# A two-layer graph network block in fp32: incidence and low-part records of the first steps made in halves

## The chip, the cores and the metric

One core of a Trainium2 chip. The time is device microseconds for one execution of the whole program; the median of several executions is compared. Five engines work beside each other and are ordered by semaphores: TensorE (PE), VectorE (DVE), ScalarE (ACT), GpSimd (POOL) and SyncE (SP, which issues most transfers).

## What is computed

For each of 16 graphs, with x of 512 x 256 and an adjacency matrix adj of 512 x 512 (all sizes fp32), two blocks follow each other, each added to its input:

```python
h = jnp.maximum(_layernorm(x), 0.0)
x = x + L0(h, adj)          # hypergraph convolution, relu, layer norm, convolution, + h
h = jnp.maximum(_layernorm(x), 0.0)
x = x + L1(h, adj)          # diffusion with attention, K = 3, relu

# inside L0
H = (adj != 0).astype(x.dtype)
w = adj.reshape(N, -1)[:, :C]
xw = jnp.einsum('ncd,hd->nch', x, W)
Dn = 1 / jnp.einsum('nce,ne->nc', H, w)          # 0 where the sum is not positive
Be = 1 / H.sum(axis=1)
m = Be[:, :, None] * jnp.einsum('nce,nch->neh', H, xw)
out = Dn[:, :, None] * jnp.einsum('nce,neh->nch', H, m) + b
```

H is the incidence matrix; the kernel needs it in two orders, as `inc` and transposed as `inct`. To keep fp32 accuracy, a factor of a product is held as a high part rounded for TensorE and a low part, the rest.

## The kernel before, in words

The work is a pipeline over the 16 graphs. Each engine runs the same steps k = -1 to 17, in `run_steps` (line 75 on); a step ends the second block of graph k - 2, does the beginning of that of k - 1 and the first block of k, and prepares k + 1. The steps k = -1, 0 and 1 are written out, k = 2 to 13 are a loop of 6 passes with two steps each (`eng.Fori`, line 86), and k = 14 to 17 are written out again. Every engine has its own copy of this loop and its own branch, recorded at L86. Nothing but semaphores ties the engines together, and the order of the work on each engine is the order in which the Python code issues it.

Step k = -1 is the opening of VectorE, `first_loads` (line 1483 on): statistics of x, then alternating one tile of `inc` (`incidence`, L1222) and one of `h_lo` (`h_lo_of`, L1476 to 1481), four of each, then the four tiles of the transposed incidence `inct` (`inct_tile`, L1485 to 1488, each as its transfer has landed), mixed with the reciprocals `be` (L1511 to 1513) and the low parts of m (`m_lo`, L1379, which write `part_b`). TensorE's `m_first` (line 1054 on) waits per tile for `inc`, for `h_hi` (made by GpSimd, L402) and for `h_lo`; its next products, at the top of step 0, wait for each tile of `inct` and of `part_b`. Step k = 0 is `first_step` (line 1529 on); it calls `h_lo_of` for four tiles, behind `y_lo` and ahead of `g_tile` (L1425), the whole `inct` of the next graph in one record (`inct_of`, L1437), the sums (L1207), `m_parts` (L1371 to 1379) and x1 (L1456). GpSimd makes `xt_lo` (L488; `g_lo` in the code, which shares its memory) behind additions of the skip term (L449).

In the loop h_lo is GpSimd's (L407), so that the changed functions are called in the steps k = -1 and k = 0 only, ahead of the loop. The first records of a pass on VectorE are those of `norm_x` (L1272 to 1287): a memset `landed` (L1279), eight `bn_aggr` into `mv_x` (L1281), two tiles of `inc`, and then `u_lo` (L1228), the low part of u, for which TensorE's products with `w_hi` and `w_lo` wait. The names `x`, `y`, `xl`, `e_sb` in the rows are x1, y10, xl or g_f, e_sb.

Of the kernel before, what the change touches and what calls it, by code (L numbers as in the profile page):

```python
# [27 lines left out]
P = 128  # L28
# [3 lines left out]
ALU = mybir.AluOpType  # L32
# [21 lines left out]
def at(s, ahead, tile=3):  # L54

    return s.k4 + (4 * ahead + tile + 1)
# [12 lines left out]
def wait(eng, sem, value):  # L69

    if not isinstance(value, int) or value > 0:
        eng.wait_ge(sem, value)
# [21 lines left out]
def build(nc, x, adj, adj_t, w1_t, b1, gamma, beta, w2_t, b2, wv_t, bv, aw, ab, wk, bk, out):  # L94
    NB, C, D = x.shape
# [8 lines left out]
    with ExitStack() as ctx:  # L104
        def sb(name, shape, dt):
            return ctx.enter_context(nc.sbuf_tensor(name, [P] + shape, dt))

        def sem(name):
            return ctx.enter_context(nc.semaphore(name))
# [8 lines left out]
        adjt_sb = sb("adjt_sb", [2, TI, C], F32)  # L118
        inc = sb("inc", [2, TI, C], F32R)
        inct = sb("inct", [2, TI, C], F32R)  # L120
        w_row = sb("w_row", [C], F32)
        h_f = sb("h_f", [TI, D], F32)
        h_hi = sb("h_hi", [TI, D2], F32R)
        h_lo = sb("h_lo", [TI, D], F32R)
# [103 lines left out]
        po_xb, h_hi_made, h_lo_made, po_skip, po_out, po_y0, po_plo, po_glo = (  # L228
            sem(n) for n in ("po_xb", "h_hi_made", "h_lo_made", "po_skip", "po_out", "po_y0",
                             "po_plo", "po_glo"))  # L230

        dv_inc, dv_inct, dv_hw, dv_a, dv_alo = (sem(n) for n in ("dv_inc", "dv_inct", "dv_hw", "dv_a", "dv_alo"))
# [13 lines left out]
        def f32(ap):  # L246

            return ap.bitcast(F32)
# [938 lines left out]
        def _(dve):  # L1187
            def step(s):
                q, o = s.par, 1 - s.par

                def stats_x(t, ahead):

                    if s.next2 if ahead == 2 else s.next:
                        if s.k == -1:
                            dve.wait_ge(ld_x0[t // 2], 16)
                        elif t == 0:
                            wait(dve, ld_x, dma_at(s, ahead - 1))
                        dve.bn_stats(st_x[:, t, :], xin[:, t, :]).then_inc(dv_stx, 1)

                def sums(t, s=s):  # L1200

                    if s.next:
                        if t == 0:
                            wait(dve, ld_wr, dma_at(s, 1))
                        wait(dve, dv_hw, at(s, 1, t - 1))
                        wait(dve, dv_inc, at(s, 1, t))
                        dve.scalar_tensor_tensor(hw[:, :], f32(inc[:, 1 - s.par, t, :]), 1.0, w_row[:, :], ALU.mult,  # L1207
                                                 ALU.mult, accum_out=dn_t[:, 0, t:t + 1]).then_inc(dv_hw, 1)
# [4 lines left out]
                def incidence(t):  # L1213

                    if s.next:
                        if s.k == -1:
                            dve.wait_ge(ld_a0[t], 16)
                        elif t % 2 == 0:
                            wait(dve, ld_a, half_at(s, 0, t // 2))
                        if t == 0:  # L1220
                            wait(dve, pe_g, at(s, -1))
                        dve.tensor_scalar(inc[:, o, t], adj_of(t), 0.0, None,  # L1222
                                          ALU.not_equal).then_inc(dv_inc, 1)
# [34 lines left out]
                def means_of_x(lo_t, hi_t):  # L1258

                    wait(dve, dv_stx, at(s, 1, hi_t - 1))  # L1260
                    dve.memset(landed_0[:, :], 0.0)
                    for t in range(lo_t, hi_t):
                        last = dve.bn_aggr(mv_x[:, t, :], st_x[:, t, :])
                    last.then_inc(dv_mvx, hi_t - lo_t)

                def shift_of_x(lo_t, hi_t):

                    wait(dve, po_rsx, at(s, 1, hi_t - 1))
                    dve.scalar_tensor_tensor(nb_x[:, lo_t:hi_t], mv_x[:, lo_t:hi_t, 0], -1.0, rs_x[:, lo_t:hi_t],
                                             ALU.mult, ALU.mult).then_inc(dv_nbx, hi_t - lo_t)  # L1270
# [105 lines left out]
                def m_lo(t):  # L1376
                    if s.next:
                        wait(dve, ac_m, at(s, 1, t))
                        dve.scalar_tensor_tensor(part_b[:, t, D:], ps0[:, t, 0:D], be[:, o, t:t + 1],  # L1379
                                                 f32(part_b[:, t, 0:D]), ALU.mult, ALU.subtract).then_inc(dv_mlo, 1)  # L1380
# [95 lines left out]
                def h_lo_of(t):  # L1476

                    wait(dve, ac_hf, at(s, 1, t))
                    wait(dve, h_hi_made, at(s, 1, t))
                    dve.tensor_tensor(h_lo[:, t, :], h_f[:, t, :], f32(h_hi[:, t, 0:D]),  # L1480
                                      ALU.subtract).then_inc(h_lo_made, 1)

                def first_loads():

                    def inct_tile(t):  # L1485
                        dve.wait_ge(ld_at0[t], 16)
                        dve.tensor_scalar(inct[:, o, t, :], adjt_sb[:, o, t, :], 0.0, None,
                                          ALU.not_equal).then_inc(dv_inct, 1)

                    stats_x(0, 1)  # L1490
                    stats_x(1, 1)
                    means_of_x(0, 2)
                    stats_x(2, 1)
                    stats_x(3, 1)
                    means_of_x(2, 4)
                    shift_of_x(0, 2)
                    incidence(0)
                    shift_of_x(2, 4)
                    h_lo_of(0)
                    incidence(1)  # L1500
                    h_lo_of(1)
                    incidence(2)
                    h_lo_of(2)
                    h_lo_of(3)
                    incidence(3)
                    inct_tile(0)
                    inct_tile(1)
                    for h in range(2):
                        pair = slice(2 * h, 2 * h + 2)
                        wait(dve, pe_m, at(s, 1, 2 * h + 1))  # L1510
                        dve.tensor_scalar(be_cnt[:, pair], ps0[:, pair, D], 1.0, None, ALU.max).then_inc(dv_bec, 2)  # L1511
                        dve.wait_ge(dv_bec, at(s, 1, 2 * h + 1))
                        dve.reciprocal(be[:, o, pair], be_cnt[:, pair]).then_inc(dv_be, 2)
                    inct_tile(2)
                    m_lo(0)
                    m_lo(1)
                    m_lo(2)
                    inct_tile(3)
                    m_lo(3)
                    dve.wait_ge(su_gb, 1)  # L1520
                    sums(0)
                    sums(1)
# [329 lines left out]
```

## Time and profile before

| | |
|---|---|
| median of 3 runs | 823.91 us (823.74 to 824.27) |
| the profiled execution | 824.95 us, of which the span of the records 823.2 us |
| mean granted TensorE clock | 0.997 of 2.4 GHz |
| TensorE busy | 806.8 us, 98% |
| VectorE busy | 640.3 us, 78%, 1740 records |
| chain that ended last | TensorE 85%, VectorE 6%, time with no cause shown 4% |

Times in the rows are microseconds from the first record. The idle time of an engine before a record stands in square brackets with what ended it; "issue" stands for no wait that the profile shows. A group of records xN that follow each other is one row, and since a record's end overlaps the next one's start, two take less than twice one. A q behind an engine's name is its sequencer, which handles branches, register operations and waits. The queue "q14 instruction" moves the program's own code.

### The profile page before, as it was taken

To read this page: it belongs to the slowest core of one execution; us is meant where nothing else is said; L and a number is where in the kernel's file an instruction comes from. 1 tells how busy PE (TensorE), PEld (TensorE's weight loads), DVE (VectorE), ACT (ScalarE), POOL (GpSimd) and SP (SyncE) were. 2 spreads that over 40 slices of the span, in tenths; PEclk is the share of its full clock that TensorE was granted. 3 is DMA by queue.
4 is the path that set the end of the run, shared out by engine and by line. 5 is a ranking of instruction groups with operands and counts; after the bars stand their busy time and mean duration, and the time that the engine had idled before them with its cause. 6 is when DMAs were issued, how large, how long until landed. Compare 5 with 4: busy or idle time off the path is not lost.

```text
span 823.2 us, 16671 instructions
## 1 busy us (share of the span) xinstructions
PE 806.8 (98%) x5750; PEld 751.5 (91%) x5750; DVE 640.3 (78%) x1740; ACT 474.6 (58%) x1005; POOL 429.6 (52%) x588
## 2 busy tenths in 40 slices
PE   7989999999999999999999999999999999999998
PEld 6878999999899989989899998998989999899997
DVE  6989878876878767878678787787877878786676
ACT  4438366572845728367383754747456483664745
POOL 2676573634738355482545736365473645832242
PEclk9999999999999999999999999999999999999999
DMA  9411204041130402204022130312204022020001
GB/s 299 124 64 52 91 15 153 2 137 32 42 124 0 166 2 76 89 0 166 2 76 90 33 133 2 121 45 76 89 2 160 6 76 90 13 91 1 26 2 52
DMA packets 39881, 58.03 MB, mean 70 GB/s; under 512 B 2576, under 2 KB 21008, under 8 KB 39824
## 3 DMA queue, kind: packets, MB, share of 16 engines
q1 hardware_dynamic: 39104, 57.42, 20.9%
q14 instruction: 40, 0.33, 0.1%
q8 instruction: 17, 0.28, 0.1%
q10 hardware_dynamic: 720, 0.01, 0.0%
HBM read 49.03 MB, written 8.39 MB: 70 GB/s over the span
## 4 chain that ended last, share of the span: by engine, by line
PE 85%; DVE 6%; issue 4%; POOL 2%; ACT 1%; DMA 1%; ACTq 0%; SPq 0%; DVEq 0%; POOLq 0%
PE ps L810 79%; PE ps L1035 3%; PE ps L965 1%; DVE x L1456 1%; PE ps L1011 1%; DVE y L1399 1%; DMA adj_sb<-in_adj 1%; DVE st_x L1462 1%; DVE inc L1222 1%; DVE part_a L1228 1%; DVE st_r L1331 1%; ACT h_f L591 0%; POOL skip L414 0%; POOL h_hi L402 0%; DVE mv_x L1281 0%
## 5 line engine op out<-in xcount | busy, mean ns | idle before, releaser
L810 PE MATMUL ps<-w_hi,part_a 128*128 128x256 f32 (+1 forms) x512 | 157.6, 342 | 6.8 <-DVE part_a L1228 4.2
L421 POOL TENSOR_TENSOR y<-y,bk_row 128x256 f32<-128x256 f32 x64 | 56.6, 914 | 199.3 <-DVE a_lo L1355 190.4
L810 PE MATMUL ps<-w_lo,part_a 128*128 128x256 f32 (+1 forms) x384 | 122.5, 319 | 0.0
L810 PEld LDWEIGHTS ps<-w_hi,part_a 128*128 128x128 f32 x512 | 96.2, 188 | 22.4 <-DVE part_a L1228 6.9
L810 PE MATMUL ps<-wk_hi,xt_hi 128*128 128x258 f32 (+1 forms) x256 | 89.4, 349 | 0.1
L810 PE MATMUL ps<-wk_hi,xt_lo 128*128 128x258 f32 (+1 forms) x256 | 86.7, 339 | 0.0
L810 PE MATMUL ps<-wk_lo,xt_hi 128*128 128x258 f32 (+1 forms) x256 | 86.6, 338 | 0.0
L810 PEld LDWEIGHTS ps<-w_lo,part_a 128*128 128x128 f32 x384 | 72.7, 189 | 5.4
L1349 DVE TENSOR_TENSOR e_sb<-e_sb,adjt_sb 128x512 f32<-128x512 f32 x64 | 44.2, 692 | 40.3 <-ACT e_sb L673 40.3
L810 PE MATMUL ps<-w_hi,part_b 128*128 128x256 f32 x256 | 72.4, 283 | 0.0
L488 POOL TENSOR_TENSOR xt_lo<-xl,xt_hi 128x256 fp32r<-128x256 f32 x60 | 56.1, 964 | 30.4 <-ACT xt_hi L747 30.4
L504 POOL TENSOR_TENSOR p_lo<-y,p_hi 128x256 fp32r<-128x256 f32 x64 | 45.6, 740 | 44.9 <-ACT p_hi L741 44.0
L741 ACT ACTIVATE p_hi<-y 128x256 fp32r<-128x256 f32 x60 | 24.0, 419 | 76.5 <-DVE y L1399 76.5
L810 PE MATMUL ps<-p_hi,a_hi 128*128 128x256 f32 x256 | 64.6, 286 | 0.0
L810 PE MATMUL ps<-y_hi,a_hi 128*128 128x258 f32 x256 | 64.4, 282 | 0.0
L810 PE MATMUL ps<-y_lo,a_hi 128*128 128x256 f32 x256 | 64.4, 282 | 0.0
L810 PE MATMUL ps<-xt_hi,inct 128*128 128x256 f32 x256 | 62.5, 285 | 1.5 <-POOL xt_lo L488 1.5
L734 ACT ACTIVATE part_b<-ps,be 128x256 fp32r<-128x256 f32 x64 | 28.4, 473 | 61.6 <-DVE be L1374 58.0
L810 PE MATMUL ps<-inct,part_b 128*128 128x512 f32 x256 | 62.5, 396 | 1.4 <-DVE part_b L1379 1.4
L810 PE MATMUL ps<-part_a,inc 128*128 128x256 f32 x512 | 62.6, 280 | 0.0
L810 PE MATMUL ps<-xt_lo,inct 128*128 128x256 f32 x256 | 62.1, 284 | 0.0
L810 PE MATMUL ps<-p_lo,a_hi 128*128 128x256 f32 x256 | 62.0, 281 | 0.0
(161 smaller groups left out, 2530.9 us busy)
## 6 DMA issues: line engine op xcount, KB each, us to landing
adj_sb<-in_adj SPq DMA_DIRECT2D x30, 512.0 KB, 5.9
adjt_sb<-in_adj_t SPq DMA_DIRECT2D x15, 1024.0 KB, 5.3
xin<-in_x SPq DMA_DIRECT2D x15, 512.0 KB, 4.6
out_dram<-x SPq DMA_DIRECT2D x15, 512.0 KB, 3.3
w_row<-in_adj SPq DMA_DIRECT2D x16, 256.0 KB, 3.5
adjt_sb<-in_adj_t SPq DMA_DIRECT2D x4, 256.0 KB, 7.1
e_sb<-in_w_t SPq DMA_DIRECT2D x2, 512.0 KB, 8.4
y<-in_wk SPq DMA_DIRECT2D x3, 256.0 KB, 7.0
```

What stands on the lines that cost most here:

```text
L421: pool.tensor_tensor(y10[:, t, D:], y10[:, t, D:], bk_row[:, :], ALU.add).then_inc(po_y0, 1)
L488: pool.tensor_tensor(g_lo[:, t, :], g_f[:, t, :], f32(g_hi[:, t, :]), ALU.subtract).then_inc(po_glo, 1)
L504: pool.tensor_tensor(p_lo[:, t, :], y10[:, t, 0:D], f32(p_hi[:, t, :]), ALU.subtract).then_inc(po_plo, 1)
L734: act.activation(part_b[:, t, 0:D], ps0[:, t, 0:D], ACT.Copy, scale=be[:, o, t:t + 1]).then_inc(ac_m, 1)
L741: act.activation(p_hi[:, t, :], y10[:, t, 0:D], ACT.Copy).then_inc(ac_p, 1)
L810: return pe.matmul(dst, stationary, moving, start=first, stop=last, skip_group_check=True)
L965: last = pe.transpose(ps0[:, t, col(2 * j + d)], xl[:, 2 * t + j, col(d)], ident[:, :])
L1011: last = pe.transpose(row[:, col(t)], column, ident[:, :])
L1035: last = pe.transpose(ps0[:, t, col(c)], r_sb[:, t, col(c)], ident[:, :])
L1222: dve.tensor_scalar(inc[:, o, t], adj_of(t), 0.0, None, ALU.not_equal).then_inc(dv_inc, 1)
L1228: dve.tensor_tensor(part_a[:, TD + d, :], ps0[:, d, :], f32(part_a[:, d, :]), ALU.subtract).then_inc(dv_ulo, 2)
L1349: dve.tensor_tensor(e_sb[:, t, :], e_sb[:, t, :], adjt_sb[:, o, t, :], ALU.mult).then_inc(dv_a, 1)
```

## The change

The low part of h in the two first steps, 128 x 256 for each tile, is subtracted in two halves of 128 columns, and each tile of the first transposed incidence, 128 x 512, is compared in two halves of 256 columns. The semaphore is raised by the second half. Four tiles of h_lo in k = -1, four in k = 0 and four of inct in k = -1: twelve records more on VectorE, all ahead of its loop. Nothing else differs.

```diff
                     wait(dve, ac_hf, at(s, 1, t))
                     wait(dve, h_hi_made, at(s, 1, t))
-                    dve.tensor_tensor(h_lo[:, t, :], h_f[:, t, :], f32(h_hi[:, t, 0:D]),
-                                      ALU.subtract).then_inc(h_lo_made, 1)
+                    for half in (slice(0, P), slice(P, D)):
+                        last = dve.tensor_tensor(h_lo[:, t, half], h_f[:, t, half], f32(h_hi[:, t, half]),
+                                                 ALU.subtract)
+                    last.then_inc(h_lo_made, 1)
 
                 def first_loads():
 
                     def inct_tile(t):
                         dve.wait_ge(ld_at0[t], 16)
-                        dve.tensor_scalar(inct[:, o, t, :], adjt_sb[:, o, t, :], 0.0, None,
-                                          ALU.not_equal).then_inc(dv_inct, 1)
+                        for half in (slice(0, C // 2), slice(C // 2, C)):
+                            last = dve.tensor_scalar(inct[:, o, t, half], adjt_sb[:, o, t, half], 0.0, None,
+                                                     ALU.not_equal)
+                        last.then_inc(dv_inct, 1)
```

## Rows read from the trace of the kernel before

**Rows 1.** The page: busy time of each engine; the instruction queue's packets.
```profile
PE 806.8 (98%) x5750; PEld 751.5 (91%) x5750; DVE 640.3 (78%) x1740; ACT 474.6 (58%) x1005; POOL 429.6 (52%) x588
...
q14 instruction: 40, 0.33, 0.1%
```

**Rows 2.** Windows, the loop's first two passes: length, busy us (records) by engine.
```profile
101.20:200.10 98.90, 98.90 (x716) 92.75 (x715) 78.67 (x214) 58.52 (x124) 53.57 (x72) 1.00 0.21 70
200.10:299.70 99.60, 99.02 (x714) 92.60 (x713) 77.73 (x213) 58.42 (x124) 53.70 (x72) 1.00 0.20 69
```

**Rows 3.** Timeline of VectorE, first record of the second pass (start, us, line, operation).
```profile
203.90 0.06 DVE L1279 MEMSET landed<- 128x1 f32 x1 [3.60 <-issue]
```

**Rows 4.** Waits of the whole span: us in total, times, longest.
```profile
DVE mv_x L1281 <- issue: 14.6, 4, 3.8
```

**Rows 5.** Timeline of VectorE, the same records inside the first pass.
```profile
151.16 0.78 DVE L1281 BATCH_NORM_AGGREGATE mv_x<-st_x 128x2 f32<-128x6 f32 x8
```

**Rows 6.** Timeline of TensorE at the start of the second pass.
```profile
206.00 0.49 PE L810 MATMUL ps<-w_hi,part_a 128*128 128x512 f32 x1 [0.58 <-DVE part_a L1228]
```

**Rows 7.** Records of line 86 from 196 to 204 us: ns, then first and last start.
```profile
L86 ACTq COMPARE_BRANCH  x1: 54/54/54, 197.5 to 197.5; - x1
L86 ACTq FUSED_REGOPS  x1: 44/44/44, 197.8 to 197.8; - x1
...
L86 DVEq COMPARE_BRANCH  x1: 72/72/72, 200.1 to 200.1; - x1
```

**Rows 8.** DMA view, windows 200.1:203.6, 203.6:206, 206:210, 250:254: packets, MB, share.
```profile
q14 instruction: 2, 0.02, 2.2%
...
q14 instruction: 1, 0.01, 1.1%
...
q14 instruction: 1, 0.01, 0.7%
...
q14 instruction: 1, 0.01, 0.9%
```

**Rows 9.** Groups by line and shape on VectorE: busy us, mean ns of one.
```profile
L1336 DVE TENSOR_TENSOR y_lo<-ps,y_hi 128x256 fp32r<-128x256 f32 x64 | 26.6, 422 | 16.7 <-ACT y_hi L602 16.4
L1228 DVE TENSOR_TENSOR part_a<-ps,part_a 128x512 fp32r<-128x512 f32 x32 | 21.8, 683 | 8.1 <-ACT part_a L558 8.1
...
L1437 DVE TENSOR_SCALAR inct<-adjt_sb 128x2048 fp32r<-128x2048 f32 x15 | 19.4, 1291 | 0.0
```

**Rows 10.** Timeline of VectorE in the step k = -1.
```profile
8.15 0.63 DVE L1480 TENSOR_TENSOR h_lo<-h_f,h_hi 128x256 fp32r<-128x256 f32 x1 [0.38 <-POOL h_hi L402]
...
9.25 0.60 DVE L1480 TENSOR_TENSOR h_lo<-h_f,h_hi 128x256 fp32r<-128x256 f32 x1
...
10.11 0.75 DVE L1480 TENSOR_TENSOR h_lo<-h_f,h_hi 128x256 fp32r<-128x256 f32 x2
...
11.12 0.75 DVE L1487 TENSOR_SCALAR inct<-adjt_sb 128x512 fp32r<-128x512 f32 x2
12.17 0.16 DVE L1511 TENSOR_SCALAR be_cnt<-ps 128x2 f32<-128x2 f32 x1 [0.30 <-PE ps L810]
```

**Rows 11.** Timeline of TensorE in the step k = -1 and at the top of step 0.
```profile
9.96 0.69 PE L810 MATMUL ps<-h_lo,inc 128*128 128x256 f32 x4
...
13.94 4.07 PE L810 MATMUL ps<-inct,part_b 128*128 128x512 f32 x16 [1.40 <-DVE part_b L1379]
```

**Rows 12.** Timelines of ScalarE and GpSimd in the step k = 0.
```profile
42.41 1.59 ACT L747 ACTIVATE xt_hi<-xl 128x256 fp32r<-128x256 f32 x4 [1.71 <-DVE xl L1425]
...
42.66 4.24 POOL L449 TENSOR_TENSOR skip<-xin,b_row 128x256 f32<-128x256 f32 x4
46.86 2.79 POOL L488 TENSOR_TENSOR xt_lo<-xl,xt_hi 128x256 fp32r<-128x256 f32 x4
```

**Rows 13.** Windows in the step k = 0; the third figure from the end is TensorE's granted clock.
```profile
47.00:50.50 3.50, 2.32 (x12) 1.69 (x13) 3.04 (x11) 2.78 (x5) 3.50 (x5) 0.99 0.63 217
50.50:53.90 3.40, 3.40 (x18) 3.40 (x17) 1.67 (x5) 0.00 (x0) 3.40 (x5) 0.50 0.22 85
```

## The prediction

> **What bounds the kernel now.** I read the page first. TensorE is busy for 98% of the span and VectorE for 78% [rows 1], so in steady state TensorE is the bound and the 12 added VectorE records cost nothing by being work. What matters is where TensorE waits. Two kinds of place are left: the opening, which runs once, and the way round the loop, which runs 6 times.
>
> The windows view, cut at VectorE's branches, gives the passes [rows 2]. In the first pass, which VectorE enters by falling into the loop, TensorE is busy all of 98.90 us. The second, entered by a jump back, has 99.60 - 99.02 = 0.58 us without a matmul. The timeline of VectorE says why: ahead of the first record of that pass stand 3.60 us that no semaphore explains [rows 3], and the list of waits has four more of the kind, 14.6 us together [rows 4]: all five jumps. The same records inside a pass, at 151.16, have no gap [rows 5]. TensorE has work queued and loses only 0.58 us, waiting for the low part of u (L1228) [rows 6]; the rest of the stall is covered.
>
> The DMA view says what the stall is. While VectorE stands still, two packets of the instruction queue are moved; one more follows as it resumes, one near 208 us, one near 251 us [rows 8]. Counting the loop's instructions in order, waits and register operations included, I get 284 per pass, about 292 records ahead of it, and these last two fetches fall about 28 and 156 instructions behind the head. They are 128 apart: the code comes in pieces of 128, the head lies 28 short of an edge, and the body covers 28 + 128 + 128 instructions, three pieces. ScalarE's body (169 instructions) covers two pieces, and its first instruction of the pass comes 0.3 us behind its branch at 197.5, where VectorE's branch at 200.1 is followed by the stall [rows 7]. So a jump finds its target still there when it goes one piece back, and not when it goes two.
>
> **The change, part by part.**
> *Length of the added records.* A subtract over 512 columns takes 683 ns and over 256 columns 422 ns [rows 9]: 0.26 us per 256 columns, and 128 columns should last 422 - 130 = 292 ns. The third and fourth h_lo together last 0.75 us where one lasts 0.41 [rows 10], so they start 0.34 us apart: 0.26 us of columns and 0.08 us fixed. A split adds one fixed part, 0.08 us. For the comparison, two of 512 columns last 0.75 us [rows 10], so 0.33 us from start to start, and 2048 columns 1291 ns [rows 9]: (1.29 - 0.42) / 3 = 0.29 us per 512 and about 0.05 us fixed. Where GpSimd works beside it, h_lo took 0.60 to 0.63 us [rows 10], so for those the fixed part is bounded by 0.05 below and 0.2 above. In all 8 x 0.08 + 4 x 0.05 = 0.84 us of VectorE, with ends of 0.5 and 2.0 us. No semaphore is raised by a first half, so no reader starts sooner.
>
> *The step k = -1 (four h_lo, four inct).* TensorE's products with h_lo(1) start at 9.96, 0.11 us behind the end of that record at 9.85 [rows 10, 11]: they go by VectorE, so the first two splits stand on the path, 2 x 0.08 = 0.16 us. h_lo(3) ends at 10.86 and is wanted after 11.4 (the four products per tile take 0.7 us from 9.96 on), which hides h_lo(2) and h_lo(3) in part; I take 0.05. VectorE idles 0.30 us before the first be_cnt at 12.17 [rows 10], which hides inct(0) and inct(1). inct(2) stands straight ahead of the part_b that ends TensorE's 1.40 us wait [rows 11]: 0.05 on the path. inct(3) is ahead of the last part_b, 0.05 more, half hidden behind the products of the others. Sum 0.3 us; with no cover it would be 0.52.
>
> *The step k = 0 (four h_lo).* They run in a row and end 0.32 us later. Behind them stand g, inct, the sums and m. What TensorE waits for is xt_lo on GpSimd, which starts at 46.86 only because four skip additions hold GpSimd from 42.66 [rows 12]; its input xt_hi is ready at 42.41 + 1.59 = 44.0. That cover is 2.9 us, against 0.32. The others feed TensorE only after its products with xt_lo, and wait under the same cover. What can show is that VectorE's longer use slows GpSimd beside it: 0 to 0.3 us, I take 0.1, as it is the same kind of neighbour that stretches h_lo from 0.42 to 0.6.
>
> *The loop.* No record of it changes, but all of it lies 12 instructions further on. The head is then some 16 short of an edge and the body covers 16 + 128 + 128 + 12, four pieces, or, should the head come to lie on the edge itself, 128 + 128 + 28, three. The jump back goes two or three pieces in either case, so the stall stays: 5 x 0.58 us for TensorE as now, nothing gained or lost. In the four-piece case one more fetch is asked for 11 instructions before the branch. Those 11 include four x1 and four statistics of 0.35 to 0.4 us each, so it is asked for some 3 to 4 us before the branch, about as long as the whole stall with two packets takes, and should cost nothing. Bounds: -0.58 us per pass (no stall) and, from the only row of a fetch, +2.6 us per pass (rival 1). Over five jumps -2.9 to +13 us; I take 0, as the count of pieces crossed is on the same side as now.
>
> *Sum.* 0.3 + 0.1 + 0 = 0.4 us. The profiled execution took 824.95 us for a span of 823.2, and would become 825.4. It stands 1.04 us above the median of the runs, 823.91, which would become **824.3**.
>
> **A rule weighed against this.** The rows show pieces of 8 KB (40 packets, 0.33 MB) at every 128th instruction [rows 1, 8]. The Trainium skill, "Runtime: NRT & Kernel Launch", section "Instruction fetch mechanics", speaks of an instruction memory of two blocks of 256 instructions for each engine but TensorE, of purely sequential prefetch, and of a taken branch that stalls when its target is outside that window. The trace agrees with the stall, not with the size of a piece. By that rule, if the edge behind the head is one of 256, the body now covers two blocks (28 + 256) and would cover three (16 + 256 + 12), with one more fetch to wait for at each jump; that is rival 1, and the sum would be its 837 instead of 824.3.
>
> **The rivals.**
> 1. *Slower: the head comes too close to the edge of what the jump fetches.* The mechanism: the two packets of the stall are one block, of which the head lies in the second half; what follows is the third packet, asked for on resuming. Now VectorE crosses the edge at about 207.3, behind a wait for GpSimd, and the piece is there. Twelve instructions sooner it crosses at about 204.5, beside the records that start with the jump [rows 3], and if a piece needs up to 3.5 us from asking (the stall itself) it is there at 203.6 + 3.5 = 207.1: up to 2.6 us of waiting ahead of u's low part, where TensorE has no slack left, times 5 = 13 us: 837. It decides as soon as the missing piece is later than 204.5. For it: nothing in the rows says which halves the two packets are. Against it: the stall waits for both packets, which makes sense if both are wanted, and only one is fetched on resuming. Chance 0.08.
> 2. *Faster: the stall shrinks or goes.* If the new position lets the jump hit, TensorE loses no 0.58 us at five jumps: 824.3 - 2.9 = 821.4. Against it: the body is longer than two pieces of 128 wherever it starts. Chance 0.14.
> 3. *Slower by the clock.* TensorE was granted 0.50 from 50.50 to 53.90, that is 1.2 GHz, and 0.99 (2.4 GHz) just before [rows 13]; before it fell, TensorE had been busy 2.32 of 3.50 us. Work at half the clock costs at most half of the 3.4 us, 1.7 us. Later work in the opening can add a second such stretch, 824.3 + 1.7 = 826.0, or lose this one, 822.6. Chance of one more 0.08, one less 0.04.
> 4. *Nothing shows:* every split hidden, 823.9. It lies in the forecast's own range.
>
> **How the numbers follow.** A measurement of this kernel can tell 0.2%, 1.65 us, from no change: outside 822.26 to 825.56. The forecast with rival 4 has 0.66, rival 1 0.08, rival 2 0.14, rival 3 0.12; of rival 3 the part with one stretch less stays within 0.2%. Faster: 0.14. Slower: 0.08 + 0.08 = 0.16, and 0.02 for the splits and contention at their upper ends, 0.18. Within: 0.68. The forecast's own range is 823.7 to 825.3 (all hidden; twice or three times my terms, towards the 2.0 us end). For 8 in 10 I go to rival 2's full gain below, 821.3, and to rival 3 with the splits' upper end above, 826.6; the 0.08 of rival 1 is left out.
>
> **What would show it.** In the changed profile: eight h_lo pairs near 0.25 to 0.4 us a record; TensorE's product with part_b(0) starting at 14.1 to 14.4, not 13.94; the gap at VectorE's jump 3.5 to 3.7 us in all five; TensorE's wait for part_a after it 0.5 to 0.8 us; instruction packets per pass five or six. The forecast is wrong if a second gap stands a few records behind the jump (rival 1), if the gap is missing or under 3 us (rival 2), or if the passes grow or shrink by more than 0.3 us.

## The result, and the profile after

The changed kernel takes **825.69 us** (median of 22 runs, 825.13 to 826.1), the kernel before 824.04 us in the same session (22 runs, 823.6 to 825.42): ratio 1.0019, interval 1.0012 to 1.0025. That is 1.65 us more, against 0.4 us in the prediction's sum; the time lies between the 821.3 and 826.6 that the prediction gave for 8 in 10, above its narrower 823.7 to 825.3, and at the edge of what it called no change (0.2%, 1.65 us). The profiled execution took 826.01 us, its span 824.2 us, 1.0 us more than the span before.

The page after, busy time and instruction queue (rows 1 are those of before):

```profile
PE 807.7 (98%) x5750; PEld 751.5 (91%) x5750; DVE 643.6 (78%) x1752; ACT 475.1 (58%) x1005; POOL 426.7 (52%) x588
...
q14 instruction: 40, 0.33, 0.1%
```

Twelve more VectorE records, as many instruction packets as before. I went on in the order of the prediction's steps.

**The opening.** Timelines of VectorE in the step k = -1, against [rows 10]:

```profile
8.25 0.72 DVE L1481 TENSOR_TENSOR h_lo<-h_f,h_hi 128x128 fp32r<-128x128 f32 x2 [0.74 <-POOL h_hi L402]
...
9.43 0.67 DVE L1481 TENSOR_TENSOR h_lo<-h_f,h_hi 128x128 fp32r<-128x128 f32 x2
...
10.37 0.88 DVE L1481 TENSOR_TENSOR h_lo<-h_f,h_hi 128x128 fp32r<-128x128 f32 x4
...
11.51 0.88 DVE L1490 TENSOR_SCALAR inct<-adjt_sb 128x256 fp32r<-128x256 f32 x4
```

Four halves together last 0.88 us where two whole ones last 0.75 [rows 10]: 0.065 us per split, near the 0.08 and 0.05 assumed. TensorE follows: its product with part_b(0) stands at 14.33 in place of 13.94 [rows 11].

```profile
14.33 0.47 PE L810 MATMUL ps<-inct,part_b 128*128 128x512 f32 x1 [1.47 <-DVE part_b L1379]
...
20.42 0.50 PE L810 MATMUL ps<-w_hi,part_a 128*128 128x512 f32 x1 [0.64 <-DVE part_a L1228]
```

Then comes something the prediction had not foreseen. The second of these two products started at 19.55 before:

```profile
19.55 0.50 PE L810 MATMUL ps<-w_hi,part_a 128*128 128x512 f32 x1 [0.22 <-DVE part_a L1228]
```

So TensorE is 0.39 us late at 14 us and 0.87 us late at 20 us. VectorE's timeline after shows the other 0.48: ahead of the second low part of u in step 0 it stands still with no semaphore to wait for, which it did not do before.

```profile
18.02 1.28 DVE L1530 TENSOR_TENSOR w_lo<-e_sb,w_hi 128x512 fp32r<-128x512 f32 x2
19.68 0.69 DVE L1228 TENSOR_TENSOR part_a<-ps,part_a 128x512 fp32r<-128x512 f32 x1 [0.37 <-issue]
```

From there to the loop the lateness stays where it is. In the step k = 0 the four h_lo take 3.35 us instead of 2.53, and TensorE's product with xt_lo, 47.63 before, comes at 48.52, 0.89 late: hidden, as predicted, though the four splits take 0.82 us more there and not the 0.32 of the prediction. The stretch at half clock [rows 13] is still there, 0.8 us later (granted clock 0.61 and 0.90 in the windows 50.50:53.90 and 53.90:58.00, where it was 0.50 and 1.00).

**The loop.** The list of waits after:

```profile
DVE landed L1279 <- issue: 10.3, 4, 2.7
DVE dn_t L1303 <- issue: 4.8, 5, 1.0
DVE mv_x L1281 <- issue: 2.5, 1, 2.5
```

Before, all five jumps cost VectorE one gap of up to 3.8 us [rows 4]. Now the gap at the jump is 2.5 to 2.7 us, and a second one of 1 us stands behind it. The timeline shows where:

```profile
203.71 0.06 DVE L1279 MEMSET landed<- 128x1 f32 x1
203.81 0.54 DVE L1281 BATCH_NORM_AGGREGATE mv_x<-st_x 128x2 f32<-128x6 f32 x7
204.27 0.73 DVE L1222 TENSOR_SCALAR inc<-adj_sb 128x512 fp32r<-128x512 f32 x2
205.92 0.17 DVE L1303 TENSOR_SCALAR dn_t<-dn_t 128x4 f32<-128x4 f32 x1 [0.92 <-issue]
```

The record at 205.92 is the 17th instruction behind the head. The DMA view of after gives one instruction packet in each of the windows 197:199, 201:203.4, 203.5:205.8, 205.8:208 and 248:250; the trace puts them at 197.80 (ahead of the branch at 200.66), 201.70 (in the first gap), 204.12 (0.62 us behind 203.50, where the sequencer's first instruction of the pass stands), 206.52 and 248.70.

What it costs TensorE is easily misread. The idle time the list shows is hardly more than before (3.2 us over five jumps, 3.1 before), because the end of a matmul is modelled. The starts tell it. Timelines of TensorE, first of before, then of after:

```profile
206.34 0.40 PE L810 MATMUL ps<-w_lo,part_a 128*128 128x512 f32 x1
206.57 0.64 PE L810 MATMUL ps<-w_hi,part_a 128*128 128x512 f32 x2
207.05 0.39 PE L810 MATMUL ps<-w_lo,part_a 128*128 128x512 f32 x1
```

```profile
207.22 0.40 PE L810 MATMUL ps<-w_lo,part_a 128*128 128x512 f32 x1
207.46 0.93 PE L810 MATMUL ps<-w_hi,part_a 128*128 128x512 f32 x2
208.22 0.40 PE L810 MATMUL ps<-w_lo,part_a 128*128 128x512 f32 x1
```

From the pair of products in the second row to the row behind it TensorE needs 0.48 us before (206.57 to 207.05) and 0.76 after (207.46 to 208.22): the second of the pair waits for the second low part of u as well, and no "idle" is shown. Measured against a pass without any gap (e2_shift28 below), the products behind the jump start 0.84, 0.80, 0.82, 0.91 and 1.03 us late before, 4.4 us in all, and 1.12, 1.30, 1.09, 1.29 and 1.07 us late after, 5.9 us: the loop costs **1.5 us** more. With the opening's 0.87 that makes 2.3 us. The profiled spans differ by only 1.0 because the profiled execution of before lost 1.4 us more further on, in three of its passes, and the one of after did not (in the one place that the list of waits shows, 0.34 us at 429.76, VectorE had waited 2.4 us for a late transfer of adj_sb; the others I did not trace). The medians differ by 1.65: less than 2.3, of which more under e1 and e4 below.

### The profile page after: what moved, and what is told of

Its sections match the earlier page's. It is cut to its first block, busy times and chain, and to the rows that moved or that the text cites. A ratio compares the mean times of both kernels' runs of the same rounds, so it can differ in the third digit from the quotient of the medians.

```text
span 824.2 us, 16683 instructions
## 1 busy us (share of the span) xinstructions
PE 807.7 (98%) x5750; PEld 751.5 (91%) x5750; DVE 643.6 (78%) x1752; ACT 475.1 (58%) x1005; POOL 426.7 (52%) x588
## 4 chain that ended last, share of the span: by engine, by line
PE 84%; DVE 8%; issue 5%; ACT 1%; POOL 1%; ACTq 0%; DVEq 0%; POOLq 0%
PE ps L810 78%; PE ps L1035 3%; PE ps L965 2%; DVE x L1456 1%; DVE inc L1222 1%; DVE y L1399 1%; PE ps L1011 1%; DVE st_x L1462 1%; DVE part_a L1228 1%; DVE st_x L1198 1%; DVE st_r L1331 1%; ACT h_f L591 0%; DVE mv_x L1281 0%; POOL skip L449 0%; DVE inct L1437 0%
```

## The experiments

Two theories of the loop went in. A *piece* is the 128 instructions that one packet of 8 KB brings by the prediction's count, and an *edge* is the border of two pieces; a loop is moved against the edges by instructions added or taken away ahead of it. *Theory A*: VectorE holds a few pieces of 128 instructions; the miss at the jump depends on how far the body reaches, in pieces, up to its branch; on a miss one piece is fetched, the next is asked for on resuming. *Theory C*, the prediction's: a jump over two pieces always misses. The tool for all of them is an instruction that only looks at a semaphore raised long ago, called a look below (two such waits in the code make one instruction, as the 12 more records of e1_shift12 for 24 waits show; 128 of them fill 9.9 us in e9_shift128, under 0.08 us each), put where VectorE idles 2.49 us in the step k = 1:

```diff
                 def p_out():

+                    if s.k == 1:
+                        for _ in range(2 * N):
+                            dve.wait_ge(ld_a0[0], 16)
                     wait(dve, pe_p, at(s, -1))
```

**Place of the loop alone.** N = 12, 28, 60 on the kernel before; and N = 16 on the changed kernel, whose loop then stands where N = 28 puts it.

> The kernel before, with 12 instructions that only look at a semaphore raised long ago, put on VectorE ahead of the row sums of the step k = 1, where VectorE idles 2.49 us. No split. It tells place from work. Theory A (a jump fetches one piece of 128 instructions, and the next is asked for on resuming): the opening is as before, TensorE at 19.55 us starts the same product as before; at the five jumps VectorE has a gap of 2.7 to 2.9 us instead of 3.5 to 3.7 and a second one of 0.9 to 1.1 us some 17 instructions behind the head; time 823.9 to 824.7 us. Theory B (the loop's second gap comes from the halves themselves): no second gap, first gap 3.5 us, 824.0. If the whole slowdown of 1.65 us were the place of the loop: 825.7.

> The same with 28 instructions, which puts the loop's head on the edge of a piece and the body into three pieces. Theory A, with the sharper claim that a jump over two pieces hits when VectorE has not looked into a fourth: no gap at any of the five jumps, TensorE's 0.55 to 0.77 us at each are gone, about 3 us less, 821 us. Theory C (three pieces are always too many, the jump over two always misses): first gap 2.8 to 3.6 us at each jump, no second gap since 128 instructions follow before the next edge, 824.0.

> The same with 60 instructions: the head 32 instructions behind an edge, the body again in three pieces, its branch in the middle of the third. Theory A: no gap at the jumps, 821 us; should the 60 looks last longer than the 2.49 us that VectorE idles there, up to 2 us are lost once. Theory C: gap of 2.8 to 3.6 us at each, 824.0 to 826.

> The changed kernel, halves and all, with 16 such instructions at k = 1, so that its loop stands where that of e2_shift28 does. It gives the halves' own cost in the opening, with the loop's place held. Theory A: 0.9 us above e2_shift28 (0.39 from the halves at k = -1, 0.48 from the wait of 0.37 us ahead of u's low part in k = 0), so about 822. Theory C: 0.9 us above e2_shift28 at 824, so about 825. If the halves cost nothing: equal to e2_shift28.

The kernel before took 823.86 us beside these four.

| | us | ratio to before (interval) |
|---|---|---|
| e1_shift12 | 824.79 | 1.001 (1.0001 to 1.0019) |
| e2_shift28 | 819.08 | 0.9944 (0.9930 to 0.9957) |
| e3_shift60 | 818.80 | 0.9938 (0.9924 to 0.9952) |
| e4_halves_shift16 | 819.73 | 0.9950 (0.9937 to 0.9964) |

Twelve looks make the changed kernel's loop without a single split. The waits of e1_shift12:

```profile
DVE landed L1279 <- issue: 7.8, 3, 2.7
DVE mv_x L1281 <- issue: 5.0, 2, 2.5
DVE dn_t L1303 <- issue: 4.9, 5, 1.1
```

Its passes lose 1.17, 1.07, 1.27, 1.36 and 1.06 us, 1.5 us more in all than before loses at its jumps. The median rose by only 0.93. In the profile of e1 the window that ran at half clock before [rows 13] ran at full clock, and the first product with part_a behind it started at 59.41 instead of 59.83:

```profile
50.50:53.90 3.40, 3.40 (x27) 3.21 (x26) 2.79 (x8) 0.00 (x0) 3.40 (x5) 1.00 0.20 77
```

But that is not why the rise is small: the runs of either kernel whose mean granted clock was 1.000 differ by 0.9 us as well (medians 824.64 and 823.74). What fits is that the median run of before also loses something behind its jumps, as its profiled run did: it stands 4.78 us above e2_shift28, where its jumps cost 4.4, and e1 stands 5.71 above, where its jumps cost 5.9. No trace of such a run was taken, so this is not shown.

With 28 looks the gap is gone. The page of e2_shift28, its window over the second pass, and VectorE's timeline at the jump:

```profile
q14 instruction: 15, 0.12, 0.0%
```

```profile
199.63:298.18 98.55, 98.55 (x714) 92.50 (x713) 78.62 (x213) 58.51 (x124) 53.47 (x72) 1.00 0.21 69
```

```profile
199.43 0.74 DVE L1465 BATCH_NORM_STATS2 st_x<-x 128x6 f32<-128x256 f32 x2
200.30 0.06 DVE L1279 MEMSET landed<- 128x1 f32 x1
```

No instruction packet is moved from 196 us to the end of the loop, 15 in the whole run instead of 40, and a pass takes 98.55 us where [rows 2] have 99.60. Windows over the same five passes, cut at TensorE's branches, for before, after and e2_shift28, one after the other:

```profile
196.71:695.22 498.51, 495.02 (x3563) 462.78 (x3562) 388.15 (x1061) 292.18 (x621) 268.75 (x360) 1.00 0.21 69
```

```profile
197.61:696.25 498.64, 495.30 (x3563) 462.31 (x3561) 389.94 (x1061) 292.42 (x621) 266.04 (x360) 1.00 0.21 69
```

```profile
196.58:689.31 492.73, 492.73 (x3563) 462.50 (x3561) 393.26 (x1061) 292.52 (x621) 267.27 (x360) 1.00 0.21 69
```

Before takes 5.8 us more than e2_shift28, 4.4 of them at the jumps and 1.4 behind them; only 3.5 were visible as idle time of TensorE. Theory C, and with it the prediction's picture of the jump, falls: this body spans three pieces and its jump over two of them hits. Theory A holds, but I had sized the gain from the idle time, at 3 us; it is 4.8 us in the medians. Run e4 gives what the halves cost with the loop's place held: 0.65 us above e2 in the medians, where 0.9 was expected. These medians mix runs that had a stretch at half clock with runs that had none (the profiled e2 had one, the profiled e4 none). Among runs of the same mean granted clock it is 0.76 us (819.62 and 818.86, at 1.000) and 0.95 us (820.07 and 819.12, at 0.998), which fits the 0.87 us of the timelines. By the medians the change's 1.65 us is thus the loop's 0.93 (e1) and the opening's 0.65 (e4), 1.58 together.

**Where exactly it tips, and the opening.** e5 puts the loop between before and e1. e6 moves it one instruction the other way (the merged record below saves two, one look adds one):

```diff
-                    for t in range(TI):
-                        h_lo_of(t)
+                    h_lo_of(0)
+                    h_lo_of(1)
+                    wait(dve, ac_hf, at(s, 1, 3))
+                    wait(dve, h_hi_made, at(s, 1, 3))
+                    dve.tensor_tensor(h_lo[:, 2:4, :], h_f[:, 2:4, :], f32(h_hi[:, 2:4, 0:D]),
+                                      ALU.subtract).then_inc(h_lo_made, 2)
```

e7 adds eight records and no halves, ahead of the first statistics (20 looks hold the loop):

```diff
+                    for i in range(8):
+                        dve.memset(spare[:, i:i + 1], 0.0)
                     stats_x(0, 1)
```

e8 has the halves at k = -1 only (`if s.k == -1` around the choice of halves, 20 looks).

> The kernel before with 5 instructions that only look at a raised semaphore, at k = 1 on VectorE, between before (0) and e1_shift12. The body now reaches 5 instructions into a fourth piece and the edge lies 23 behind the head. Theory A (one piece fetched on a miss, the next asked for on resuming and usable some 2.3 us later): the fetch of the fourth piece starts about 1 us ahead of the branch, so the gap at the jump shrinks to 2.7 to 3.1 us as in the changed kernel, and VectorE reaches the edge 23 behind the head only 2.2 us after resuming, so the second gap is nearly gone (0 to 0.3 us). TensorE then loses 0.1 to 0.4 us per jump in place of 0.8 to 1.0 (before) and 1.1 to 1.3 (after): 820.5 to 822.5, so better than both. Theory D (every position that misses costs the same): 824.0 to 824.8.

> The kernel before with its loop 1 instruction earlier: in k = 0 the subtract of h_lo(2) and h_lo(3) is one record over both (2 instructions fewer, in a stretch that waits for GpSimd anyway), and 1 look at k = 1. The branch that closes the loop is then the last but one slot of its third piece, where in the kernel before it is the last. Theory A with the sequencer looking one instruction ahead: no gap at the jumps, 819.1 as e2_shift28. If it looks two or more ahead: gap of 3.5 us, 824.0. Theory E (the kernel before misses because its head is far into a piece, not because of where its branch lies): 824.0.

> The kernel before with 8 small memsets of a spare tile ahead of the first statistics of k = -1, where VectorE waits for x until 3.78 us, and 20 looks at k = 1, so that the loop stands where that of e2_shift28 does. No halves: the records of k = -1 and 0 take as long as before but lie 8 further on. It asks whether the wait of 0.37 us ahead of u's low part (k = 0) in the changed kernel comes from the place of the code. If from the place (edge of a piece right ahead of that record): that wait is there, TensorE is 0.48 us later from 20 us on but not at 13.94, time 819.5 (0.5 above e2_shift28's 819.1). If from the halves' own length: no such wait, 819.1.

> Halves only at k = -1 (four h_lo, four inct: 8 more records), none at k = 0; 20 looks at k = 1 hold the loop where e2_shift28 and e4_halves_shift16 have it. If the halves at k = 0 are hidden, as predicted: equal to e4_halves_shift16, 819.7, with TensorE 0.39 us later from the product with part_b(0) and 0.87 us from 20 us on. If the halves at k = 0 cost what VectorE spends on them (0.8 us): 0.3 to 0.8 us below e4_halves_shift16.

The kernel before took 823.74 us beside these.

| | us | ratio to before (interval) |
|---|---|---|
| e5_shift5 | 819.72 | 0.9951 (0.9937 to 0.9965) |
| e6_shift_minus1 | 819.09 | 0.9945 (0.9932 to 0.9959) |
| e7_early8 | 819.56 | 0.9949 (0.9936 to 0.9963) |
| e8_halves_first_step | 819.81 | 0.9956 (0.9943 to 0.9970) |

e6: one instruction earlier, and the gap is gone at all five jumps, with 15 instruction packets. So the kernel before misses because its branch is the very first position that touches the fourth piece (it stands in the last place of the third piece, and the instruction behind it is the first of the fourth). e5: the jump misses, but the list of waits shows why it hardly costs anything:

```profile
DVE landed L1279 <- issue: 12.6, 5, 2.7
...
DVE dn_t L1308 <- issue: 0.4, 1, 0.4
```

The first gap is short as in the changed kernel, since the packet for the fourth piece is moved 2.4 us ahead of the branch and no longer beside the one for the head, and the second is almost gone, since VectorE gets to the edge, 23 behind the head, when the piece is just there. TensorE loses 0, 0, 0.16, 0 and 0.16 us. The cost of a position is not a step but a curve: 0 for -1, 0.9 us per jump for 0, 0.1 for +5, 1.2 for +12.

e7: the wait in straight code comes from the place. VectorE's timeline, with no halves anywhere:

```profile
17.68 1.28 DVE L1532 TENSOR_TENSOR w_lo<-e_sb,w_hi 128x512 fp32r<-128x512 f32 x2
19.35 0.69 DVE L1229 TENSOR_TENSOR part_a<-ps,part_a 128x512 fp32r<-128x512 f32 x1 [0.39 <-issue]
```

TensorE is 0.1 us late at 14 us and 0.54 at 20 us, and the time is 0.48 us over that of e2 (of another session, whose kernel before took 0.12 us more). The place can also be counted. I take VectorE's records in order from the first, its sequencer's included, and go back in steps of 128 from the edge that e6 found at the loop's branch: an edge lies ahead of the 64th record. In the changed kernel, e4, e7 and e8 the 64th is this low part of u, with 0.37 to 0.39 us ahead of it; in the kernel before, e1, e2, e3, e5, e6, e9, e10 and e12 it is a small record of dn_t at 20.9 to 21.3 us, and u's low part has no such gap. (In e11, below, it is the other low part of u.) e8: 819.81 beside e4's 819.73, so the four splits at k = 0 cost nothing that shows.

**Period, nearness, and two more versions.** N = 128 and N = 14 on the kernel before; the changed kernel with four early memsets and 12 looks; and the opposite of the change, one record over all four tiles of h_lo at k = 0 with six instructions fewer:

```diff
-                    for t in range(TI):
-                        h_lo_of(t)
+                    wait(dve, ac_hf, at(s, 1, 3))
+                    wait(dve, h_hi_made, at(s, 1, 3))
+                    dve.tensor_tensor(h_lo[:, :, :], h_f[:, :, :], f32(h_hi[:, :, 0:D]),
+                                      ALU.subtract).then_inc(h_lo_made, 4)
```

> The kernel before with 128 looks at k = 1: its loop lies exactly one piece of 128 further on. It asks whether the places repeat every 128 instructions or every 256. If every 128 (theory A, pieces of 128): the gap of 3.5 us stands at all five jumps as in the kernel before, no second gap, TensorE 0.8 to 1.0 us later per jump; the looks themselves last about 7 us where VectorE idles 2.49, so once up to 4.5 us are added: 824 to 828.5. If every 256: no gap at the jumps, 819 to 823.6.

> The kernel before with 14 looks: the head 14 instructions short of the edge, two nearer than in e1_shift12. Theory A: the first gap 2.7 us, the second some 15 instructions behind the head and a little longer (1.0 to 1.3 us), TensorE 1.1 to 1.5 us later per jump: 824.8 to 825.5. If the head is put on the edge itself when it comes this near to it: no gap at all, 819.1.

> The changed kernel, all halves, with 4 small memsets ahead of the first statistics of k = -1 and 12 looks at k = 1, so that the loop stands where that of e4_halves_shift16 does and all records of the opening lie 4 further on. If the wait of 0.37 us ahead of u's low part comes from the place of the code alone, the edge now falls ahead of the second product with w_row before it or the subtract for w1_lo, where VectorE has little slack either: the wait moves to one of them. If it then hides: no such wait, TensorE 0.4 us later than before from 20 us on instead of 0.87, 819.3. If it shows there as well: 819.7 as e4_halves_shift16.

> The other way round from the change: in k = 0 the four subtracts of h_lo are one record over all four tiles (6 instructions fewer), nothing else. The loop comes 6 instructions earlier, its branch 7 slots short of the end of its third piece. Theory A: no gap at any jump, 819.1 (818.7 to 819.5), better than both kernels. If only a position at the very edge of a piece hits: 824.0.

These four ran on a chip where the kernel before took 825.05 us, so their ratios count.

| | us | ratio to before (interval) |
|---|---|---|
| e9_shift128 | 832.34 | 1.0089 (1.0073 to 1.0105) |
| e10_shift14 | 833.73 | 1.0093 (1.0059 to 1.0127) |
| e11_halves_early4 | 820.02 | 0.9941 (0.9927 to 0.9955) |
| e12_merged_h_lo | 819.53 | 0.9938 (0.9924 to 0.9952) |

e9 behaves at the jumps as the kernel before does. Its waits:

```profile
DVE ri_t L1395 <- issue: 40.4, 14, 9.9
DVE landed L1279 <- issue: 11.0, 3, 3.8
DVE mv_x L1281 <- issue: 7.4, 2, 3.8
```

Five long gaps and no second one; TensorE loses 1.02, 1.06, 0.91, 0.82 and 0.82 us. The places repeat every 128 instructions. The total missed its bracket because of the looks and the clock: the looks make a gap of 9.9 us instead of 2.49 in the step k = 1, more than the 7 I had allowed, TensorE stands idle for 4.95 us, and behind that its clock falls to the lower level for 6.8 us, so that 16 products with inct take 6.81 us instead of 3.89. Both are paid once:

```profile
105.00:111.80 6.80, 6.17 (x15) 4.83 (x16) 6.65 (x27) 2.19 (x5) 3.97 (x6) 0.50 0.00 0
```

e10 was the largest miss of the experiments: I expected the second gap to grow by 0.1 to 0.3 us, and the time by 1 us. Timeline of VectorE, then windows of TensorE behind the jump (the third figure from the end is the granted clock):

```profile
202.88 0.55 DVE L1281 BATCH_NORM_AGGREGATE mv_x<-st_x 128x2 f32<-128x6 f32 x7
205.10 0.78 DVE L1222 TENSOR_SCALAR inc<-adj_sb 128x512 fp32r<-128x512 f32 x2 [1.67 <-issue]
```

```profile
205.20:207.20 2.00, 0.02 (x2) 0.02 (x1) 2.00 (x7) 0.00 (x0) 2.00 (x4) 1.00 0.02 4
207.20:210.60 3.40, 3.40 (x10) 2.66 (x11) 3.40 (x10) 2.69 (x6) 1.36 (x3) 0.62 0.00 0
210.60:214.00 3.40, 3.40 (x15) 2.71 (x14) 2.14 (x5) 2.02 (x4) 3.15 (x6) 0.88 0.00 0
```

Two instructions nearer, the edge stands ahead of the incidences and no longer behind them. In e1 these 0.7 us of work are done while the piece is on its way; here they come after it, and the first dn_t lasts 0.68 us instead of 0.17. TensorE then idles 2.0 us, and behind that idle time its granted clock fell to the lower level (0.50, 1.2 GHz) from 208.0 to 211.4 us, and likewise behind the other four jumps. TensorE's first product starts 2.1 to 2.2 us late, and in the stretch at half clock it loses 1.6 us more: 3.8 us per jump in the profiled run, whose time was 837.97 and whose mean granted clock was 0.990. Of the four runs two were like it (836.41 too), and two took 831.05 and 829.92 us with a mean granted clock of 0.998, too high for five such stretches. So the clock does not fall behind every such jump.

e11 moved the wait in straight code and did not remove it: with all records four further on it stands ahead of the other low part of u, where it is lumped with a wait for ScalarE.

```profile
17.74 0.69 DVE L1229 TENSOR_TENSOR part_a<-ps,part_a 128x512 fp32r<-128x512 f32 x1 [0.72 <-ACT part_a L559]
```

e12, with no padding at all, takes 5.5 us less than the kernel before on the same chip (0.6%), and so is faster than both kernels, as e2, e3 and e6 are.

## Why the prediction was right, and where not

**The splits: right.** The sum had 0.3 us for k = -1, measured 0.39 at 14 us; 0.1 for k = 0, measured nothing (e8 beside e4), under the cover of GpSimd's additions that the prediction named. Together 0.4, as put. VectorE's own extra time at k = 0 was mis-sized, 0.82 us and not 0.32; the cover of 2.9 us hid either.

**The range: right by luck.** The total of 0.4 us was a quarter of the 1.65 measured, and two parts of that, the loop and the wait in the opening, the sum had at nothing. The time fell inside 821.3 to 826.6 because its upper end had been set for a second stretch at half clock, which did not come. By the prediction's own signs the forecast was wrong: a second gap stands behind each jump, and the first is under 3 us.

**The opening's other 0.48 us: missed.** The prediction spoke of the code's place for the loop only. Twelve (here the first eight) more records also move the edges of pieces through the straight code ahead of it, and one came to stand ahead of a record for which TensorE waits. That the place is the cause was shown by e7, which has it without the halves, and by the count of the 64th record in all runs; what VectorE waits for there is not shown, as no instruction packet is moved in that gap.

**The loop, taken at 0: wrong, it is +1.5 us by the traces (+0.93 in the medians, e1).** The step that failed is the inference from [rows 7, 8] that "a jump finds its target still there when it goes one piece back, and not when it goes two". With it the count of pieces could change nothing. The counting itself was right (284 instructions, edges 28 and 156 behind the head, a fourth piece entered after the change), and so was the reasoning that the packet asked for ahead of the branch is harmless; it even shortened the first gap. The mechanism that decided is rival 1, given 0.08: the edge came so near to the head that VectorE met it before the piece was there. The observable named for it, a second gap a few records behind the jump, is in the profile at all five. Its bound was 2.6 us per pass and the gap 0.92, since VectorE went on 2.3 us after it had resumed (203.50 to 205.83, where the sequencer's next record stands; 1.7 us after the packet at 204.12), not 3.5; that is why the time stayed at the edge of no change and did not go to 837. e10 shows that two instructions more would have gone most of that way, to 833.73.

**Rival 2: dismissed for a wrong reason.** Against it stood that the body is longer than two pieces wherever it starts. That holds, and does not matter: three pieces fit. 28 instructions instead of 12 give rival 2's case, and more than its 2.9 us.

**The price of a jump was read too low.** The prediction took TensorE's idle time, 0.58 us [rows 6], for the loss. By e2 it is 0.84 there, and 4.4 us over five jumps instead of the 2.9 of the sum (3.1 in the list of waits).

**Rival 3: neither sign in the changed kernel.** The stretch at half clock moved with the work. In the profiled e1 it was absent (as in e3 and e4, but not in e2), and TensorE was then 0.42 us ahead; the 1.7 us of the prediction was a bound, and four times that.

**The rule weighed.** The trace shows, by e9 and e6, that the places repeat every 128 instructions and that a body of 284 stays resident as long as it touches three pieces. The Trainium skill, "Runtime: NRT & Kernel Launch", section "Instruction fetch mechanics", has two blocks of 256 instructions. The size of the store, 512 instructions, would fit four pieces of 128 with one fetched ahead; the period of 256 does not fit e9. By that rule e9, moved by half a block, need not have behaved as the kernel before did; it did, and the measurement decides.

## What to carry to other kernels

When an edit adds or removes instructions ahead of a loop, on the engine that runs it, count where the loop's head and its branch fall in pieces of 128 and time the edit with that place held (padding in a slack spot, as in e4) before saying what the edit itself costs: here the place was worth from -5 to +9 us and the edit 0.65 (0.87 by the timelines, 0.48 of it again by a place, that of an edge in the opening). And measure a stall by how late the waiting engine's next starts are against a pass without it, not by the idle time printed beside them.

## What the runs showed that I had not expected

- A loop of 284 VectorE instructions runs with no instruction fetch at all when it touches three pieces of 128, and with five packets per pass and a gap of 2.5 to 3.8 us at each jump when its branch touches the fourth; one instruction decides (e6 beside the kernel before, 819.09 and 823.74 us).
- The cost per jump as the loop moves by -1, 0, +5, +12, +14 and +28 instructions is 0, 0.9, 0.1, 1.2, 3.8 and 0 us of TensorE's time in the profiled runs (of the 3.8, 1.6 are half clock). Places between +14 and +28 were not tried.
- Behind 2.0 us without a matmul TensorE's granted clock fell to 0.50 for 3.4 us at each jump of the profiled e10, but not in all its runs; behind the 4.95 us of e9 it fell for 6.8 us; behind the 0.5 to 0.9 us of the other kernels' jumps it did not fall.
- In straight code an edge in front of a critical record cost VectorE 0.37 to 0.39 us and TensorE 0.48 us, once.
